# Last expert layer: gate and up in halves over three PSUM banks, two banks for turned rows, the f16 split on VectorE, indirect DMAs in pairs

## What is computed

```python
tidx, tw = _route(x, router_weight, e_bias)          # 4 of 16 experts
g = jnp.einsum('th,eih->tei', x, gate_w)
u = jnp.einsum('th,eih->tei', x, up_w)
h = jax.nn.silu(g) * u
yo = jnp.einsum('tei,ehi->teh', h, down_w)
combine = jnp.zeros((T, E), tw.dtype).at[jnp.arange(T)[:, None], tidx].add(tw)
routed = jnp.einsum('te,teh->th', combine, yo)
shared = _mlp(hidden_states.reshape(-1, H), sh_gate_w, sh_up_w, sh_down_w)
return (routed + shared).reshape(orig_shape)
```

## Time and profile before

| | |
|---|---|
| median of 3 runs | 1928.43 us (1925.21 to 1930.17) |
| span of the profiled execution | 1908.7 us |
| TensorE, matmuls busy | 1651.9 us, 87% |
| VectorE busy | 1188.1 us, 62% |
| ScalarE busy | 1005.9 us, 53% |
| GpSimd busy | 763.4 us, 40% |
| first matmul of the loop over groups (L2040) | 1485.6 us after the span's start |
| start of the last one | 1816.1 us |

### The profile page before, as it was taken

How to read it: one execution, slowest core, us unless ns; L and a number is a source line. 1 busy time by engine, 2 the same in 40 slices (tenths; PEclk the granted TensorE clock), 3 DMA queues, 4 the chain that set the end, 5 groups by cost and what they waited for, 6 DMA issues and landing times. The chain is left out here.

```text
span 1908.7 us, 44330 instructions
## 1 busy us (share of the span) xinstructions
PE 1651.9 (87%) x16920; PEld 1256.1 (66%) x16920; DVE 1188.1 (62%) x2667; ACT 1005.9 (53%) x1744; POOL 763.4 (40%) x932
## 2 busy tenths in 40 slices
PE   4699999758999999999995899999886898888885
PEld 3355666437888888888883566665643777776753
DVE  4678887735555565565566788777762556345546
ACT  4377877635445444444433456645544576555541
POOL 2155657875310101000036334423651535565534
PEclk9699999978999999999997999989997999999898
DMA  9753333214645544544224434423243456677523
GB/s 288 208 117 68 72 60 68 57 41 133 203 150 196 172 139 167 195 158 135 67 84 107 99 80 79 71 55 58 76 125 144 164 200 233 232 235 250 190 90 121
DMA packets 297700, 256.99 MB, mean 135 GB/s; under 512 B 198047, under 2 KB 270155, under 8 KB 296216
## 3 DMA queue, kind: packets, MB, share of 16 engines
q1 hardware_dynamic: 271256, 168.84, 32.5%
q0 software_dynamic: 26240, 85.32, 13.4%
HBM read 102.98 MB, written 107.74 MB: 110 GB/s over the span
## 5 line engine op out<-in xcount | busy, mean ns | idle before, releaser
L1643 PE MATMUL ps<-m_xT,m_w_halves 128*128 128x256 f16 x3360 | 413.9, 273 | 2.2 <-issue 2.2
L1643 PEld LDWEIGHTS ps<-m_xT,m_w_halves 128*128 128x128 f16 x3360 | 329.4, 98 | 41.4 <-issue 2.8
L1158 ACT ACTIVATE a_probs<-ps 128x1024 f32<-128x1024 f32 (+1 forms) x256 | 234.8, 917 | 183.8 <-PE ps L995 181.9
L1662 PE MATMUL ps<-m_w_halves,m_hiddenT 128*128 128x256 f16 x1680 | 229.8, 273 | 5.1 <-DVE m_hiddenT L1758 4.6
L1274 POOL TENSOR_TENSOR a_probs<-a_probs,a_half_above 128x512 f32<-128x512 f32 x128 | 162.3, 1270 | 157.2 <-ACT a_probs L1158 156.6
L1719 ACT ACTIVATE m_hiddenT<-m_hidden 128x256 f16<-128x256 f32 x280 | 116.6, 416 | 197.6 <-DVE m_hidden L1755 191.6
L1758 DVE TENSOR_TENSOR m_hiddenT<-m_hidden,m_hiddenT 128x256 f16<-128x256 f32 x280 | 119.2, 426 | 135.1 <-ACT m_hiddenT L1719 130.7
L1610 POOL DMA_DIRECT2D expert_out<-m_y x40 | 28.9, 722 | 434.8 <-DVE m_y L1738 432.2
L2162 ACT ACTIVATE m_rowsT<-ps 128x1024 f16<-128x1024 f16 x112 | 115.9, 1035 | 154.0 <-remote 93.8
L1357 DVE TENSOR_REDUCE a_qT<-ps 128x4 f16<-128x1024 f32 x128 | 156.5, 1223 | 51.1 <-PE ps L1006 50.2
L1662 PEld LDWEIGHTS ps<-m_w_halves,m_hiddenT 128*128 128x128 f16 x1680 | 163.5, 98 | 26.9 <-DVE m_hiddenT L1758 7.2
(11 more groups left out here) (319 smaller groups left out, 3070.3 us busy)
## 6 DMA issues: line engine op xcount, KB each, us to landing
routed<-m_zeros POOLq DMA_DIRECT2D x32, 768.0 KB
r_space<-routed SPq DMA_DIRECT2D x48, 512.0 KB
routed_out<-m_y SPq DMA_DIRECT2D x48, 512.0 KB
r_w_load<-in_L_w SPq DMA_DIRECT2D x24, 896.0 KB
dispatched<-r_xT SPq DMA_DIRECT2D x10, 1024.0 KB, 6.6
expert_out<-m_y POOLq DMA_DIRECT2D x40, 256.0 KB
a_ctx_in<-in_ctx SPq DMA_DIRECT2D x32, 256.0 KB
m_experts_load<-in_L_experts SPq DMA_DIRECT2D x18, 384.0 KB, 3.5
```

The lines of the kernel that those rows point to most:

```text
L1158: A(pr[:, g % 2, 2 * jp:2 * jp + 2, :], SC[:, :, 0:SPAN], ACT.Exp, scale=1.0 / math.sqrt(DH)).then_inc(asem["ex"], 1)
L1643: last = mm(psum[:, v % HB, m * CH:(m + 1) * CH], wh[:, u, ws_, m, d_ * F0 + f_ * P:d_ * F0 + (f_ + 1) * P], xT[:, q % XB, xs_ * KT + d_, ...
L1662: last = mm(psum[:, 4 + 2 * (q % 2) + t, 0:D], hT[:, hs_, f_, t * P:(t + 1) * P], wh[:, u, ws_, 2, f_ * D:(f_ + 1) * D], start=f_ == 0 and ...
```

## The change

In the loop over groups:

- Gate and up of half a group take one bank, and halves go round banks 0, 1 and 2 (`half_gate_and_up`). Silu and product are done by halves, 128x256.
- Turned rows of a first half stay in bank 5, those of a second half go to bank 3. A turning waits for the copy of the same half of the group before, not for the last copy.
- The upper f16 half is made by VectorE, in `split_hidden`, in front of the subtraction; ScalarE's `upper_hidden` is gone, in the shared jobs too.
- POOL issues two indirect DMAs when a group's first half of turned rows is there (`xp_done`), and two when the second is.
- ScalarE copies down's results between the first silu and the second copy of turned rows.

The core of the diff:

```diff
-        rows_turned = psum[:, 5, :].bitcast(F16)
+        def rows_turned(l, half):
+            return psum[:, 3 if half and L0 < l <= L1 else 5, :].bitcast(F16)
...
+        def half_gate_and_up(n):
+            parts = psum[:, n % 3, :].rearrange("p (t m f) -> p t m f", t=2, m=2)
+            return parts[:, :, 0, :], parts[:, :, 1, :]
...
                 for r in range(NR):
-                    pool.wait_ge(h_done, H0 + U0 + r)
-                    for what, b, begin, first, end in PACED:
-                        j = first + (r - begin) * PER_GROUP
-                        if first <= j < end:
-                            what_of = scatter if what == "scatter" else gather
-                            what_of(b, j, min(j + PER_GROUP, end))
+                    for half in range(2):
+                        pool.wait_ge(xp_done, 2 * (L0 + r + 1) + half + 1)
+                        for what, b, begin, first, end in PACED:
+                            j = first + (r - begin) * PER_GROUP + half * (PER_GROUP // 2)
+                            if begin <= r and j < end:
+                                what_of = scatter if what == "scatter" else gather
+                                what_of(b, j, min(j + PER_GROUP // 2, end))
...
-                    if l or half:
+                    if L0 < l <= L1:
+                        if half and l == L0 + 1:
+                            pe.wait_ge(g_done, H0 + through(U0 - 1))
+                        else:
+                            pe.wait_ge(xp_out, 2 * (l - 1) + (1 if l == L0 + 1 else half) + 1)
+                    elif l == L1 + 1 and half == 0:
+                        pe.wait_ge(xp_out, 2 * (l - 1) + 1)
+                    elif l or half:
                         pe.wait_ge(xp_out, 2 * l + half)
...
                 def routed_hidden(r, half, experts):
-                    q, l = U0 + r, L0 + r
+                    l, n = L0 + r, 2 * r + half
                     pe.wait_ge(xp_out, 2 * l + half + 1)
-                    if half == 0:
-                        pe.wait_ge(g_done, H0 + q - 1)
+                    pe.wait_ge(g_done, H0 + U0 + n - 2 if n >= 3 else H0 + U0 - 1 + n // 2)
...
-                    if half:
-                        last.then_inc(h_done, 1)
+                    last.then_inc(h_done, 1)
...
-                for r in range(NR + 1):
-                    if r:
-                        silu(U0 + r - 1)
+                for r in range(NR):
                     take_rows(L0 + r + 1, 0)
-                    if r:
-                        upper_hidden(U0 + r - 1)
+                    half_silu(r, 0)
                     routing_before(r)
-                    take_rows(L0 + r + 1, 1)
                     if r >= 2:
                         evict(r - 2)
+                    take_rows(L0 + r + 1, 1)
+                    half_silu(r, 1)
                     routing_behind(r)
...
+                    V.tensor_copy(dst[:, q % 2, 0, :], hp[:, q % 2, :]).then_inc(hh, 1)
                     dve.wait_ge(hh, H0 + q + 1)
                     V.tensor_tensor(dst[:, q % 2, 1, :], hp[:, q % 2, :], dst[:, q % 2, 0, :], ALU.subtract)\
                      .then_inc(hl, 1)
...
                     if r:
-                        product(U0 + r - 1)
-                        lower_hidden(U0 + r - 1)
+                        half_product(r - 1, 1)
+                        split_hidden(U0 + r - 1)
+                    if r < NR:
+                        half_product(r, 0)
                     routing_piece(r)
                     if r in PAIR_AT:
                         combine(PAIR_AT[r])
```

More of the change, by code:

```diff
@@ L1853, in gate_and_up, with half_of @@
             pair = psum[:, 2 * (q % 2):2 * (q % 2) + 2, :]
-            if U0 <= q < U1:
-                parts = pair.rearrange("p b (t m f) -> p (b t) m f", t=2, m=2)
-                return parts[:, :, 0, :], parts[:, :, 1, :]
             return tuple(pair[:, m, :].rearrange("p (t f) -> p t f", t=QT) for m in range(2))
+        def half_gate_and_up(n):
+            parts = psum[:, n % 3, :].rearrange("p (t m f) -> p t m f", t=2, m=2)
+            return parts[:, :, 0, :], parts[:, :, 1, :]
+        def half_of(t, half):
+            return t[:, half * 2 * P:(half + 1) * 2 * P].rearrange("p (t f) -> p t f", t=2)
         def by_tile(t):
@@ L1983, in turn_rows @@
                         for k in range(2 * KT):
-                            last = tr(rows_turned[:, (2 * k + t) * P:(2 * k + t + 1) * P],
+                            last = tr(rows_turned(l, half)[:, (2 * k + t) * P:(2 * k + t + 1) * P],
                                       tile[2 * half + t][:, k * P:(k + 1) * P], ident16[:, :])
@@ L1991, in shared_hidden @@
                     pe.wait_ge(w_in[0], 16)
-                    if q >= 2:
-                        pe.wait_ge(g_done, H0 + q - 1)
+                    if q >= U1 + 2 or 2 <= q < U0:
+                        pe.wait_ge(g_done, H0 + through(q - 2))
+                    elif q >= U1:
+                        pe.wait_ge(g_done, H0 + through(U1 - 1) - 1 + i)
                     for m in range(2):
@@ L2039, in routed_hidden @@
                                     .rearrange("p a (m c n) -> p (a m) c n", m=2, c=KT)[:, :, d_, :]
-                                last = mm(psum[:, 2 * (q % 2) + half, t % 2 * 2 * P:(t % 2 + 1) * 2 * P],
+                                last = mm(psum[:, n % 3, t % 2 * 2 * P:(t % 2 + 1) * 2 * P],
                                           xd[:, l % 2, xs_ * KT + d_, t * P:(t + 1) * P], both,
@@ L2267, in product, with half_product, split_hidden @@
                      .then_inc(g_done, 1)
-                def lower_hidden(q):
-                    dst = hm if U0 <= q < U1 else hT
+                def half_product(r, half):
+                    q, n = U0 + r, 2 * r + half
+                    dve.wait_ge(s_done, H0 + U0 + n + 1)
+                    dve.wait_ge(hl, H0 + q - 1)
+                    V.tensor_tensor(half_of(hp[:, q % 2, :], half), half_gate_and_up(n)[1], half_of(hsb[:, q % 2, :], half),
+                                    ALU.mult).then_inc(g_done, 1)
+                def split_hidden(q):
+                    dst = hm if U0 <= q < U1 else hT
+                    dve.wait_ge(g_done, H0 + through(q))
+                    if U0 + 2 <= q < U1:
+                        dve.wait_ge(t_done, q - U0 - 1)
+                    if q < U0 or q >= U1:
+                        l = q // 2 if q < U0 else L1 + (q - U1) // 2
+                        if l:
+                            dve.wait_ge(y_done, 2 * l)
+                    V.tensor_copy(dst[:, q % 2, 0, :], hp[:, q % 2, :]).then_inc(hh, 1)
                     dve.wait_ge(hh, H0 + q + 1)
@@ L2304, in products_of_job, with split_hidden_of_job @@
                     product(unit_of_job(j, 1))
[L2306 to L2308 removed]
+                def split_hidden_of_job(j):
+                    split_hidden(unit_of_job(j, 0))
+                    split_hidden(unit_of_job(j, 1))
                 def routing_piece(r):
```

53 lines of the change are left out of this document (20 added, 33 removed).

## The result

The change takes 1901.38 us (median of 4 runs, 1895.25 to 1904.33) against 1927.5 us for the kernel before on the same chip: a ratio of 0.987, 95% interval 0.9842 to 0.9899. That is some 26 us faster. The median lies outside the forecast range (1904 to 1943), on the fast side by under 3 us, and far from the forecast 1925.4.

A forecast was written before the change was run, and what follows sets the result against it. The prediction took POOL's loop of four indirect DMAs, which hold back TensorE's completions, as the bound. Terms -4.4 - 0.6 - 1 + 1.6 + 1.7 - 0.3 = -3.0 us took 1928.4 to 1925.4 us; range 1904 to 1943.

The forecast's parts named there:

- The loop and its hold: POOL's scatter groups: four indirect DMAs 4.81 us, completion seen 1.04 later, next start 0.87 later, 6.72 us in all.
- -4.4: 22 scatter groups before the combining: DMAs in pairs take 0.2 us less each, as some pairs slip in before the hold.
- Groups 7 and 8 without DMAs: Groups 0, 7 and 8: VectorE's routing work sets the pace; -0.3 us each for the shorter split chain, -1 in sum.
- The six gather groups: Six gather groups before the combining: DMAs in pairs take 0.1 us less each, -0.6 us.
- The 17 combining groups: Groups from 31 on, where VectorE also combines: +0.2 us for each of 8 pairs of groups, +1.6; ends -4 and +8.
- Rival B: Each pair of DMAs pays its own hold: 8.3 us a scatter group, 6.7 a gather group; 1966 or 1941 us; chance 0.18.
- Rival A: The single bank for turned rows was the bound: its 33.5 us wait goes, 1895 us, or 1912 with half; chance 0.24.
- My bound on the traffic: Against rival A: gather groups move 254 GB/s at 6.27 us; 5.5 us would need 290, so 5.25 would not be reached.
- Rival C: VectorE's cast blocks one POOL DMA a group for 0.4 us in 45 groups, +18: 1943 us; chance 0.10.
- The lower end that the prediction itself gives the pairs: Scatter groups: four DMA starts 1.28 us apart, 5.12 us, -1.6 a group.
- the case's lower end of 1916: The prediction's own case, forecast 1925.4 us, had ends 1916 and 1933; chance 0.48.
- The closing jobs: Six closing jobs: two VectorE casts before each combine, two such steps on the path, +1.7 us; upper end +2.8.

The follow-up runs named there:

- cast_undone: The change with the upper f16 half of the routed groups made by ScalarE again, all else kept: 1900.19 us, ratio 0.989 to the kernel before.
- before_paced_end: The kernel before with the last four gathers of part 2 behind the first closing unit's gate and up: ratio 0.9946.
- early_paced_end: The kernel before with the loop's combines from pair 1 one group earlier and the last four gathers paced, batches of four kept: ratio 0.9892.
- before_again: Second profile of the unchanged kernel before, on the same chip as others of its set: span 1916.1 us, ratio 0.9988.
- plain_scatter: The kernel before with part 3's scatter by plain POOL DMAs of the same bytes, sorting left out, for measuring alone: ratio 0.992.
- before_four_first: The kernel before with all four indirect DMAs of a group behind the first half of the next group's turned rows: ratio 1.0148.

## Why the prediction was wrong

- **The loop and its hold: right.** In the scatter groups the change does what the prediction said: pairs merge into four in a row, and successive batches start 6.60 us apart (forecast 6.4 to 6.7):

```profile
1646.71 0.97 POOL L748 DMA_INDIRECT routed<-m_x_halves,r_routed_row  x1 [1.74 <-PE ps L2004]
1647.99 1.04 POOL L748 DMA_INDIRECT routed<-m_x_halves,r_routed_row  x1 [0.30 <-issue]
1649.34 0.98 POOL L748 DMA_INDIRECT routed<-m_x_halves,r_routed_row  x1 [0.31 <-issue]
1650.62 0.98 POOL L748 DMA_INDIRECT routed<-m_x_halves,r_routed_row  x1 [0.30 <-issue]
1653.31 0.97 POOL L748 DMA_INDIRECT routed<-m_x_halves,r_routed_row  x1 [1.72 <-PE ps L2004]
```

  From (17) to (25), the eight groups of that scatter, the change takes 51.3 and 51.6 us instead of 53.9 and 54.7, -0.3 to -0.4 each, where -0.2 was charged. For all groups up to 29 the forecast was -6.0 (its terms -4.4, -0.6 and -1); the two pairs of profiles give -1.0 and -9.8, too far apart to judge the sum. Two of its small terms can be read. Groups 7 and 8 without DMAs, (5) to (7), charged with -0.6, take 11.9 us in both profiles instead of 13.2; cast_undone gives back 0.8 of that, which fits the shorter split chain that was the reason given. The six gather groups, charged with -0.6, got slower instead: (15) to (17) and (25) to (29) together take 3.3 and 2.4 us more in the two pairs of profiles.
- **The step that failed** is "*The 17 combining groups* ... I take +0.2 for each of 8 pairs, +1.6; ends -4 ... and +8". Measured: -10.4 and -14.0 from (29) to (44), beyond the lower end, and the sign was wrong. I read the combine as a release of POOL, 0.78 us after its end, and priced hand-overs of half a microsecond around it. The rows held more: POOL had been idle for 3.50 us in front of that gather, and the groups took 7.29 us where the same gathers without combines took 6.27. That excess, 17 x 1.02 = 17 us, was there to be asked about, and I never did. It is the closed loop of 14.73 us shown above, in which the four DMAs behind one combine hold the completions that the next combine needs. In the change two DMAs stand there:

```profile
1754.09 3.62 DVE L2309 SCALAR_TENSOR_TENSOR x_res<-m_gathered,r_gather_weight,x_res 128x256 f32<-128x256 f32 x8
...
1755.92 0.95 POOL L1930 DMA_INDIRECT m_gathered<-routed_out,r_routed_row  x1 [1.07 <-DMA routed_out<-m_y]
...
1758.80 0.43 DVE L2292 CAST m_hidden_halves<-m_hidden 128x512 f16<-128x512 f32 x1
...
1759.05 0.99 POOL L1930 DMA_INDIRECT m_gathered<-routed_out,r_routed_row  x1 [0.92 <-remote]
...
1760.35 0.95 POOL L1930 DMA_INDIRECT m_gathered<-routed_out,r_routed_row  x1 [0.30 <-issue]
...
1762.05 1.02 ACT L2182 ACTIVATE m_rowsT<-ps 128x1024 f16<-128x1024 f16 x1 [0.25 <-PE ps L2004]
...
1762.29 0.95 POOL L1930 DMA_INDIRECT m_gathered<-routed_out,r_routed_row  x1 [0.99 <-PE ps L2004]
...
1766.93 3.62 DVE L2309 SCALAR_TENSOR_TENSOR x_res<-m_gathered,r_gather_weight,x_res 128x256 f32<-128x256 f32 x8
```

  The combine ends at 1757.71, and the gather that needs it starts at 1759.05, when the turned rows are seen (POOL had been idle for 0.92 us) and not when the combine ends. From one combine to the next it is 12.84 us.
- **A term that was missing:** the end of the loop, -5.6 and -5.1 us. I had not seen the eight gathers in a row there. Pairs break them up; a later gate for the last four alone gives 22.6 us for 26.5 and 25.9 (before_paced_end), with the earlier combines 20.3 (early_paced_end).
- **Rival B's mechanism is there, at a lower price.** In the gather groups each pair does pay its own hold: 1759.05 to 1761.30 for the pair, 0.75 until the rows are seen, 0.24 to the next pair, 3.24 us, twice a group. I had priced it at 6.7 a group; it is 6.4 to 6.5, against 6.27 for fours (6.36 to 6.40 in before_again).
- **Rival A fell.** The wait at L1984 went, as said, and next to nothing came of it: with the banks and without the pairs the ratio is 0.9981. That the measured 1901 lies between A's 1895 and 1912 is luck; its mechanism isn't what gained. My bound on the traffic (290 GB/s as a hindrance) was wrong too: plain_scatter moved 295.
- **Rival C fell.** The gather at 1759.05 started 0.25 us into the cast and took 0.99 us, the next one, beside no cast, 0.95; over the loop the nine gathers that started within a cast took 0.97 to 1.01 us, and of eight scatters seven took 1.04 to 1.21 instead of 0.97. That is 17 DMAs and not one in each of 45 groups, and taking the cast off VectorE again gained nothing (cast_undone, 0.989). The Trainium skill (page "SBUF — State Buffer", section "SBUF: two separate sides") has the DMA held until the copy ends; here that end came 0.18 us after the gather's start, and the gather took 0.04 us more than the next.
- **The range.** The lower end that the prediction itself gives the pairs, -1.6 a scatter group, is -35 us for 22 groups, and neither the case's lower end of 1916 nor the range holds it; the range did not follow from its own terms.
- **Sizes.** The cast takes 0.442 us (forecast 0.42), a half product 0.419 (0.421), half a silu 0.386 (0.377):

```profile
L2280 DVE TENSOR_TENSOR m_hidden<-ps,m_silu 128x256 f32<-128x256 f32 x96 | 40.3, 419 | 35.1 <-ACT m_silu L2195 17.5 <-issue 16.1 <-DVE m_hidden_halves L2294 1.4
...
L2195 ACT ACTIVATE m_silu<-ps 128x256 f32<-128x256 f32 x96 | 37.0, 386 | 20.1 <-remote 15.4 <-PE ps L2061 4.7
...
L2292 DVE CAST m_hidden_halves<-m_hidden 128x512 f16<-128x512 f32 x48 | 21.2, 442 | 1.6
```

  The closing jobs became 3.6 and 2.6 us longer, against +1.7 with an upper end of +2.8; the two profiles of before differ by 2.9 there.

## What to carry to other kernels

Where a stretch is slower than its neighbour with the same transfers, ask for the excess a group before pricing the edit: here 7.29 against 6.27 us pointed at a loop that no single wait names. Follow each wait of the pacing engine until it closes on itself; a consumer that frees a buffer, the batch it releases, and the completions that this batch holds back were one loop, and a smaller batch or an earlier consumer opens it equally well (95.5 and 94.7 us), but not both at once (104.1, the earlier combine on the change). Ask of a gate, too, whether the batch behind it delays it: that cost 1.5% in before_four_first.

## What the runs showed of the hardware

- In these traces TensorE's completions reach the other engines late beside POOL's indirect DMAs, until 0.11 to 1.10 us after the last of them in the rows shown, and TensorE goes on starting its own work there. Plain DMAs of the same bytes from POOL (2.13 us for four, against 4.8 for four indirect ones) left a copy 0.03 us behind its transposes and TensorE busy for 39.31 of 40 us.
- ScalarE's and VectorE's completions were not held: within 0.01 us beside either kind of DMA in plain_scatter.
- What a hold delays includes the events on which POOL itself waits, so the batches form by themselves: gates on four separate events came out as twos and fours.
- The same four DMAs behind turned rows instead of gate and up made the kernel 1.5% slower (gathers without a combine start 7.8 us apart instead of 6.3 to 6.4), since that gate stands behind a held copy.
